# Eight of the 64 weight pieces are split between the prologue's tiles instead of in the last four attention units

## What is computed

```python
mod = (_silu(c) @ wmod).reshape(8, 6, 1, -1)
sa, ca, ga, sb, cb, gb = ...            # ga, gb: sign kept, magnitude at least 0.25
h = _layernorm(x) * (1 + ca) + sa
x = x + ga * attention(h, Wq, bq, Wk, bk, Wv, bv, Wo, bo, token_positions)   # causal, RoPE, softmax
h = _layernorm(x) * (1 + cb) + sb
x = x + gb * ffn(h, switch_w, switch_b, w1, b1, w2, b2)                      # argmax expert, gelu, times its probability
```

## Time and profile before

| | before |
|---|---|
| median of three runs | 781.2 us (778.49 to 782.25) |
| profiled execution | 779.62 us, span 777.9 us |
| prologue's tiles, from the first projection to the first maxima product | about 16.7 to 52.5 us |
| attention units 0 to 31 | about 65 to 497 us |
| rest of the attention part | to 518.8 us |
| routed part | 518.8 to 777.9 us |
| busy: PE, DVE, ACT, POOL | 86%, 76%, 67%, 62% |

### The profile page before, as it was taken

How to read it: one execution, slowest core, us unless ns; L and a number is a source line. 1 busy time by engine, 2 the same in 40 slices (tenths; PEclk the granted TensorE clock), 3 DMA queues, 4 the chain that set the end, 5 groups by cost and what they waited for, 6 DMA issues and landing times. The chain is left out here.

```text
span 777.9 us, 21258 instructions
## 1 busy us (share of the span) xinstructions
PE 672.6 (86%) x7438; PEld 424.9 (55%) x7438; DVE 588.5 (76%) x1215; ACT 521.0 (67%) x1061; POOL 478.9 (62%) x635
## 2 busy tenths in 40 slices
PE   5766888899999999999999888765999999999993
PEld 4432444445454544545445443444787878788772
DVE  6567888888888988888888767348577777777774
ACT  2334889899989989989899888642444444444441
POOL 4422566788878888888988777832245454535331
PEclk9797999999999999999999999956999999999997
DMA  8102423335444443634424446349566651323000
GB/s 266 38 8 49 124 89 103 102 107 146 123 139 136 140 140 109 162 111 133 137 86 153 120 146 149 121 149 369 193 214 197 215 167 59 90 83 91 31 20 0
DMA packets 61364, 97.49 MB, mean 125 GB/s; under 512 B 8405, under 2 KB 42318, under 8 KB 60753
## 3 DMA queue, kind: packets, MB, share of 16 engines
q1 hardware_dynamic: 56272, 79.36, 33.3%
q0 software_dynamic: 4992, 16.79, 6.8%
HBM read 69.47 MB, written 34.51 MB: 134 GB/s over the span
## 5 line engine op out<-in xcount | busy, mean ns | idle before, releaser
L1165 DVE TENSOR_REDUCE row_max<-ps_max 128x2 f32<-128x768 f32 (+2 forms) x192 | 200.0, 1042 | 39.5 <-PE ps_max L676 39.4
L959 ACT ACTIVATE prob<-ps_sc 128x1024 f32<-128x1024 f32 (+1 forms) x192 | 169.7, 884 | 45.9 <-PE ps_sc L703 45.3
L1515 PE MATMUL ps_h<-tok_t,w_all 128*128 128x128 f16 x1872 | 156.1, 219 | 0.7 <-DVE tok_t L1690 0.5
L1515 PEld LDWEIGHTS ps_h<-tok_t,w_all 128*128 x1872 | 130.8, 98 | 41.7 <-issue 2.2
L1585 ACT ACTIVATE hid<-ps_h,b_t 128x128 f32<-128x128 f32 x312 | 88.9, 368 | 96.1 <-PE ps_h L1515 96.1
L1432 POOL DMA_INDIRECT slot_mem<-row_dram,token x39 | 55.6, 1426 | 120.4 <-DVE y L1725 100.5
L445 POOL TENSOR_SCALAR_AFFINE_SELECT prob<-prob 128x512 f32<-128x512 f32 x128 | 86.1, 672 | 60.7 <-ACT prob L959 59.8
L1528 PE MATMUL ps_y<-w_all,hid_parts 128*128 x312 | 118.0, 379 | 1.9 <-DVE hid_parts L1700 1.6
L669 PE MATMUL ps_max<-k_t,q_t 64*128 64x512 f16 (+3 forms) x512 | 68.8, 305 | 35.6 <-DVE row_max L1165 35.1
L716 PE MATMUL ps_pv<-prob,v_sb 128*32 128x512 f32 (+3 forms) x1024 | 88.8, 442 | 0.3
L1530 PE MATMUL ps_y<-w_all,hid_parts 128*128 x312 | 85.0, 273 | 0.0
(11 more groups left out here) (269 smaller groups left out, 1362.9 us busy)
## 6 DMA issues: line engine op xcount, KB each, us to landing
raw<-w SPq DMA_DIRECT2D x64, 256.0 KB, 3.0
w_dram<-halves SPq DMA_DIRECT2D x64, 256.0 KB, 3.3
w_all<-w_dram SPq DMA_DIRECT2D x20, 512.0 KB, 4.8
row_dram<-rows SPq DMA_DIRECT2D x32, 256.0 KB, 3.4
w_all<-w_dram SPq DMA_DIRECT2D x3, 2048.0 KB, 13.5
mod_rows<-mods_dram SPq DMA_DIRECT2D x16, 256.0 KB, 7.1
row_dram<-mods_dram SPq DMA_DIRECT2D x32, 128.0 KB, 4.8
xs<-x SPq DMA_DIRECT2D x24, 128.0 KB, 3.2
```

The costliest lines, as they stand in the source:

```text
L959: nc.scalar.activation(p_kb[:, :, first * L:(first + n) * L], ps_sc[:, :, 0:n * L], ACT.Exp, scale=SCALE).then_inc(exp_done, 1)
L1165: nc.vector.tensor_reduce(dst, ps_max[:, :, 0:n * L].rearrange("p j (m l) -> p j m l", m=n), AX.X, ALU.max).then_inc(max_done, 1)
L1515: last = mm(o, w[:, :, k, f, :][:, bass.ds(e, 1), :].rearrange("p e m -> p (e m)"), tok_t[:, j % 2, piece, k, :], start=(n == 0 and f % HF ...
```

## The change

Pieces 0 to 7 are split in the prologue, two each in tiles 1 to 4: on ACT after `hi_parts(T)`, on POOL at the end of the tile's turn. SP issues their stores and the loads of pieces 2 to 9 in one run, after `load_xs(12)` and ahead of the wait for the modulation rows. Unit U then does pieces 8 + 2U and 9 + 2U, at the places at which it did 2U and 2U + 1, and units 28 to 31 do none. The number of pieces, their size and their two buffers stay as they were.

```diff
--- before.py
+++ after.py
@@ -45,6 +45,9 @@
 WARM_EARLY = 6
 WARM_LATE = 60
 PIECE = F // 2
+PIECES = 8 * E
+LEAD_PIECES = 8
+PIECE_UNITS = (PIECES - LEAD_PIECES) // 2
 X_AT = 1
 
 
@@ -357,6 +360,9 @@
                 load_piece(m)
             for T in range(2 * QT, 3 * QT + 1):
                 load_xs(T)
+            for m in range(LEAD_PIECES):
+                load_piece(m + 2)
+                store_piece(m)
             sp.wait_ge(mods_kept, 1)
             sp.wait_ge(gates_done, 1)
             sp.dma_start(mods_dram.rearrange("g b d -> b g d"), mod_r).then_inc(gates_saved, 16)
@@ -365,16 +371,19 @@
                 load_gate(b)
                 load_mods(b)
             for U in range(NU):
-                if 2 * U + 2 < 2 * NU:
-                    load_piece(2 * U + 2)
-                store_piece(2 * U)
+                m = LEAD_PIECES + 2 * U
+                if m + 2 < PIECES:
+                    load_piece(m + 2)
+                if U < PIECE_UNITS:
+                    store_piece(m)
                 if U >= STORE_LAG:
                     store_rows(U - STORE_LAG)
                 if U + 3 * QT + 1 < NT:
                     load_xs(U + 3 * QT + 1)
-                if 2 * U + 3 < 2 * NU:
-                    load_piece(2 * U + 3)
-                store_piece(2 * U + 1)
+                if m + 3 < PIECES:
+                    load_piece(m + 3)
+                if U < PIECE_UNITS:
+                    store_piece(m + 1)
                 spread_gate(U)
                 if 2 * QT <= U + 1 < NT:
                     load_xr(U + 1)
@@ -389,7 +398,7 @@
                 store_rows(X)
             for m in range(2):
                 sp.wait_ge(rows_stored[m], 16 * (NT // 2))
-                sp.wait_ge(w_stored[m], 16 * NU)
+                sp.wait_ge(w_stored[m], 16 * PIECES // 2)
             sp.wait_ge(gate_rows_saved, 16 * NT)
 
         @block.gpsimd
@@ -522,6 +531,9 @@
                 low_h(T + 1)
                 if T + 2 <= LEAD:
                     rstd_of(T + 2)
+                if T:
+                    low_piece(2 * T - 2)
+                    low_piece(2 * T - 1)
 
             for U in range(NU):
                 T = U + LEAD
@@ -535,13 +547,15 @@
                 if T + 1 < NT:
                     rstd_of(T + 1)
                 clear_future(U, 1)
-                low_piece(2 * U)
+                if U < PIECE_UNITS:
+                    low_piece(LEAD_PIECES + 2 * U)
                 clear_future(U, 2)
                 clear_future(U, 3)
                 if U == NU - 1:
                     for X in range(NT - QT + 1, NT):
                         add_const(X)
-                low_piece(2 * U + 1)
+                if U < PIECE_UNITS:
+                    low_piece(LEAD_PIECES + 2 * U + 1)
                 if U >= QT + 1:
                     row_power(U - QT - 1)
                     row_hat(U - QT - 1)
@@ -989,6 +1003,9 @@
                 if T + 1 < LEAD:
                     high_h(T + 1)
                 hi_parts(T)
+                if T:
+                    high_piece(2 * T - 2)
+                    high_piece(2 * T - 1)
             keep_kt(LEAD - 1, ps_a[:, :])
             high_h(LEAD)
 
@@ -1014,13 +1031,14 @@
                     if s == 3 and T < NT:
                         keep_v(T, ps_a[:, :], U if U % G == G - 1 else None)
                         hi_parts(T)
-                    if s == 2:
-                        high_piece(2 * U)
+                    if s == 2 and U < PIECE_UNITS:
+                        high_piece(LEAD_PIECES + 2 * U)
                     if s == 4 and X >= 0:
                         keep_att(X, ps_nd)
                     if s == 4 and T + 1 < NT:
                         normalise(T + 1)
-                high_piece(2 * U + 1)
+                if U < PIECE_UNITS:
+                    high_piece(LEAD_PIECES + 2 * U + 1)
                 if V < NU:
                     keep_shift(V)
             keep_u(NU - 1)
```

## The result

The changed kernel takes 788.28 us (median of 7 runs, 784.78 to 789.77) against 781.31 for the kernel before: a ratio of 1.0083 [1.0057, 1.011], 7.0 us slower. In a later series of 12 runs it took 785.78 against 780.95: 1.0068 [1.0044, 1.0093], 4.8 us slower. The forecast was 785.9, 4.7 slower. The runs of one kernel fall into two groups, and TensorE's granted clock goes with them: of the 12 runs eight lie between 785.1 and 787.0 and four between 790.2 and 791.9, and the four have the lower mean clock (0.940 to 0.947 against 0.951 to 0.954).

What follows compares the result with a forecast made beforehand. No engine is full; the chain of waits lies in the untouched routed part, whose start shifts. Prologue +6.9, unit ends -1.1 and tail -1.1 sum to +4.7 us on the median of 781.2: 785.9, range 782 to 790.

Steps and rivals of the forecast that it cites:

- What bounds it: Whole kernel: no engine full, waits chain in the untouched routed part; only prologue, unit ends 28 to 31 and tail count.
- Pieces 0 and 1: Prologue, tile 1: loaded at the start, covered while tile 2's projection is awaited; cost nothing, 2.4 us on ACT if uncovered.
- Pieces 2 and 3: Prologue, tile 2: transfers queue behind load_xs(12), ACT waits for load 2 and store 0; rotate(3) 6.0 us late.
- Pieces 4 and 5: Prologue, tile 3: waits for stores 2 and 3 add 0.9 us, making rotate(4) 6.9 us late.
- bounds of 5.5 and 8.5: Prologue stall in all: 5.5 us with the shortest landings, 8.5 with stores landing after 4.1 us.
- Pieces 6 and 7: Prologue, tile 4: cost nothing, covered by ACT's 9.62 us of idle time before keep_shift(0).
- First exponential: Start of unit 0: nothing is added behind rotate(4), so unit 0's maxima begin 6.9 us later.
- Units 28 to 31 and the tail: Last units: 0.37 us gained at three unit ends, 1.1 in all, and 1.1 more after the last unit.
- The clock: Rival: PE's longer prologue wait drops its clock, unit 0's maxima take 2.8 us more, 788.7 us; chance 0.25.
- Units 0 to 27: nothing: Units 0 to 27: each does two pieces in the same places with the same four DMAs, so no change.
- step "sum": Whole kernel: +6.9 in the prologue, -1.1 at unit ends, -1.1 after the last unit, +4.7 us.

Runs made afterwards that it cites:

- e3_gain_alone: Kernel before without its last eight pieces; units 28 to 31 split nothing, expert 6's weights are loaded for expert 7's: 780.31 us (0.9987).
- f1_before_busy: Kernel before with small unused products in PE's waits of units 27 and 31: 779.97 us (0.9985).
- e2_repeat_last: Changed kernel, but units 28 to 31 split pieces 0 to 7 a second time: 790.54 us (1.0118).
- e4_keep_warm: Changed kernel with 70 and 45 small unused products ahead of PE's waits at tiles 3 and 4: 785.76 us (1.0074).
- f2_after_busy: Changed kernel with small unused products in PE's waits of units 27 and 31: 785.18 us (1.0065).
- after_second: Changed kernel again, unedited, in the series of the pure delay, with a second profile: 785.78 us.
- delay_act: Kernel before with ten repeated high halves on ACT behind hi_parts(2), a pure delay: 785.27 us (1.0058).
- late6_busy: Changed kernel with six early pieces, their transfers before x's last loads, four placed behind the tile chain, small products in units 27 and 31: 779.34 us (0.9984).
- lead4_busy: Four early pieces, 2 and 3 behind ACT's last high_h and POOL's last tile, small products in units 27 and 31: 778.23 us (0.9974 against before).

## Why the prediction was right

*What bounds it* held: the routed part took 259.00 us before and 259.50 after (258.68 to 260.48 over all profiles), and the three places named are where the edits acted.

*Pieces 0 and 1* cost nothing, as said. Their low halves stand directly ahead of `rotate(2)`, which began at 33.81, 0.78 later than in `e3_gain_alone`, but `load_xs(12)` went out at 37.55, against 37.50 there.

*Pieces 2 and 3.* The stall has the forecast's form: SP's pairs directly behind `load_xs(12)`, ACT idle for 5.20 us (about 5 forecast) until store 0 lands, the low halves ahead of `rotate(3)`. The times by the span's clock are 1.7 to 2.8 us lower than forecast because this execution ran the early tiles at full clock and issued `load_xs(12)` 3.0 earlier. From the issue of `load_xs(12)` piece 2 began after 4.5 us (4.3 forecast) and `rotate(3)` after 8.6 (8.0).

*Pieces 4 and 5.* `rotate(4)` came after 15.65 us, 14.3 forecast. Mis-sized is the landing of the stores: 3.3 was used, and ACT was released 3.6 us after the issue of store 0, 4.2 after that of store 1 and 4.05 after that of store 3. So the stall in the tiles is 6.9 + 1.3 = 8.2 us in the profiled execution, inside the bounds of 5.5 and 8.5. The other 2.0 us to the first exponential are clock: 1.0 from `rotate(4)` to the first maxima product (5.56 us; 4.56 before) and 1.0 in the maxima.

*Pieces 6 and 7* were covered, as said: ACT is idle for 10.64 us before `keep_shift(0)`.

*First exponential.* By the table it stands at 64.4 to 65.2 us in the three profiles with the old prologue (before, `e3_gain_alone`, `f1_before_busy`) and at 71.2 to 74.6 in the five with the early split (after twice, `e2_repeat_last`, `e4_keep_warm`, `f2_after_busy`): means of 64.9 and 72.2, 7.3 apart, 6.9 forecast. From the issue of `load_xs(12)` it came after 26.9 us in `e3_gain_alone` and `f1_before_busy`, whose early tiles also ran at full clock, and after 33.7 to 34.9 in `f2_after_busy`, `e2_repeat_last`, `e4_keep_warm` and the kernel after. That this is so close to the forecast is in part luck: beside `e3_gain_alone` `rotate(4)` is 7.5 late, and the old prologue loses about as much to the clock behind its own `rotate(4)` (6.07 us to the first maxima product, 5.56 in the kernel after), a loss that the forecast had in neither.

*Units 28 to 31 and the tail.* 0.36 at each of three unit ends against the forecast's 0.37. `row_power(26)` came 11.55 us after unit 31's first exponential in `f2_after_busy` and 12.69 in `f1_before_busy`: 1.14 at the very step, 1.12 forecast. To the routed part it is 1.45 (30.94 - 29.49); the other 0.3 lie behind the step, and the forecast doesn't explain them. So 2.2 to 2.5 in all, 2.2 forecast. By the medians it was 2.3 (`e2_repeat_last`) and 0.2 (`e3_gain_alone`); the second is the miss, which a fall in unit 31 would explain as far as its one profile goes.

*The clock.* The rival had the wrong price, and its cause isn't shown. After 7.08 us of PE's wait the clock was 0.50, but in `e3_gain_alone` it fell within the same projection after a wait of 2.15, so the longer wait need not be what brought it. In the kernel after it was 0.50 again in unit 0's maxima; there it cost 1.0 us, not 2.8. That the first median, 788.28, lies near this rival's 788.7 is luck: in the profile most of the excess lies in units 27 and 31. The Trainium skill ("TensorE: Matmul & The Clock Gate", HAM oscillation) names a mechanism, a wait between groups of products after which the next runs at half rate; the trace agrees at 46.50, and not at the 3.40 us wait of the earlier trace rows.

*Units 0 to 27: nothing* was wrong for this execution, by what the trace shows not through the pieces but through the clock. The span grew by 10.2, 5.5 more than the sum; of that 2.4 lie in unit 27 and 2.3 in unit 31 and the tail (1.2 longer instead of 1.1 shorter); the rest is 0.4 ahead of the first exponential and 0.5 in the routed part.

So the step "sum" was right by two of three pairs of medians (785.18 - 779.97 = +5.2 with the small products, +4.8 in `after_second`), and its terms by the profiles. The first median's further 2 us fit the falls of the clock in units 27 and 31, but they are not shown to be these: the products there take 3.1 us from that median, 0.6 from the second one, and 0.8 from the kernel before's. Whether the clock falls there more often in the changed kernel, and why, stays open. The one profile of the kernel before has no such fall, but `delay_act`, which splits no piece early, had one in both units. A later start of the units alone did not raise the total beyond itself, and no run took the early transfers and the pieces in unit 27 apart for this.

## What to carry to other kernels

Idle time of an engine is usable only where its work's inputs have landed and nothing of the chain stands behind it in the queue: look where the transfers are issued, since a run of loads placed behind a waiting load inherits its wait. Move side work to the end of a chain's section rather than between its links, and look which engine works beside it there. Where a kernel's times spread, compare versions with the clock held at the places where it falls, before a gain of 1 or 2 us is called lost.

## What the runs showed of the hardware

A DVE operation of 0.41 us on float32 in place, `TENSOR_SCALAR`, took 1.26 while POOL's subtraction ran, and ended 0.28 us behind it; another took 0.89 instead of 0.42 and also ended 0.28 behind POOL's. The Trainium skill ("SBUF — State Buffer", Who interferes with whom) says that VectorE's `tensor_scalar`, in a mode that uses two ports, and GpSimd exclude each other for a whole instruction; the trace agrees: the same 0.28 us were left behind POOL's end whether DVE had begun 0.31 or 0.54 after POOL, as if it had stood still beside it. Which mode the operation ran in stands in no row.

Groups of 8 and 14 small products in PE's waits left the granted clock at 1.00 through units 27 and 31 in all four profiles that had them (`f1_before_busy`, `f2_after_busy`, `late6_busy`, `lead4_busy`), while without them it fell in at least one of the two units in eight of nine profiles (not in that of the kernel before). Each is one execution. The 70 products ahead of tile 4 in the prologue, behind which PE still waited 3.98 us, did not hold it there (0.51 from 46 to 52 us).
